# Three copies of turned attention blocks, made by ScalarE instead of VectorE, in a two-layer gated cross-attention kernel

## The chip, the core and the metric

The kernel runs on one core of one Trainium2 chip. A core has TensorE (PE in the rows; its weight loads are PEld), VectorE (DVE), ScalarE (ACT), GpSimd (POOL) and SyncE (SP, which issues most of the DMAs). Each engine works through its own list of instructions in order and waits on semaphores that other engines raise. The metric is device time in microseconds (us) of one execution, the median of several runs.

## What is computed

Two layers over `x` (2 batches, 256 rows, 128 columns), each with cross-attention to a context of 2 x 512 rows and then a feed-forward part:

```python
x = x + tanh(g_xattn[0]) * L0_xattn(layernorm(x), ctx, mask)   # 16 heads of depth 8
x = x + tanh(g_ffn[0])   * L0_ffn(layernorm(x))                # Hadamard turn, rows quantised to 4 bits, ternary weights
x = x + tanh(g_xattn[1]) * L1_xattn(layernorm(x), ctx, mask)   # 16 heads of depth 64
x = x + tanh(g_ffn[1])   * L1_ffn(layernorm(x))                # 32 experts, top 4 of them, and a shared one
```

`xattn` is `softmax(mask(q k^T / sqrt(depth))) v`, projected out. All of it is in float32.

## The kernel before

**Units.** The attention is cut into 128 units, numbered u = 0 to 127: one head, 128 query rows, all 512 context rows. Units 0 to 63 are the first layer (8 blocks of 8 units; four blocks are one batch), units 64 to 127 the second (16 blocks of 4 units). One unit passes through these steps:

1. PE computes the scores into one of two PSUM banks (`scores`, L1352 in the first layer, L1358 and L1359 in the second). Score u waits until the mask step of unit u-2 has emptied the bank.
2. DVE adds the mask and takes the row's extreme (`mask_max`, L941, two instructions); its result lies in one of three slots, so mask step u waits for the exponential of unit u-3.
3. ACT takes the exponential with its row sum (`exp`, L747, two instructions).
4. DVE takes the reciprocal of the sums (`recip`, L950).
5. POOL multiplies the rows by it (`norm`, L604).
6. PE turns the block, four 128x128 transposes into one PSUM bank (`turn`, L1227). The first layer has three such banks, so turn u waits for the copy of unit u-3.
7. The turned block is copied from PSUM into `probsT` (`copy_turned`), by DVE (L958) or by ACT (L756).

When the units of a block are copied, PE multiplies them with the values (`mix`, L1396). Below, "copy 40" is step 7 of unit 40, "mask step 40" its step 2, and so on.

**The order.** All of this is written out by hand as one list for each engine, from a loop over a step t. At step t PE makes score t+6, the jobs that `PLAN` has for t, a mix if one is due, and then turn t. DVE makes mask step t+5, reciprocal t+3, the jobs of t-1, and copy t-1 if it is DVE's; behind these come the feed-forward part and the norms. ACT makes the jobs of t-1, the exponential t+4, and copy t-1 if it is ACT's. POOL multiplies unit t+3 and has conversions, splits and norm rows behind that.

**Who copies.** Odd units are copied by ACT, even ones by DVE, except for those in a list, which ACT copies too (lines 167 and 176 to 178):

```python
MORE_ON_ACT = (36, 46, 48, 68, 70, 78, 80, 102, 110, 112)
...
def on_act(u):
    return u % 2 == 1 or u in MORE_ON_ACT
```

**The work around the change.** At t = 6 DVE has the statistics of the first norm for the second batch (`ln_stats`, L911 to L914) at the end of its step. The feed-forward part of the first batch lies at t = 37 to 47: at t = 38 its norm's statistics, at t = 41 `quantise` part 0 (L1036 to L1043, six small instructions, one behind the other), at t = 42 part 1 (L1045 to L1050). PE has mix 0 (block 0) at t = 10, mix 4 at t = 42 and mix 5 at t = 50, each ahead of that step's turn. The second layer's first projections begin at t = 49 (`k_high` by ACT, L798).

Of the kernel before, what the change touches and what calls it, by code (L numbers as in the profile page):

```python
# [163 lines left out]
BEFORE, PLAN, AFTER, NUMBER, PLACE, HIGHS = make_plan()  # L164


MORE_ON_ACT = (36, 46, 48, 68, 70, 78, 80, 102, 110, 112)
GATE_SLOTS = 4
RING = 3
LAG = 3  # L170
# [4 lines left out]
def on_act(u):  # L175

    return u % 2 == 1 or u in MORE_ON_ACT

# [1415 lines left out]
```

## Time and profile before

| | |
|---|---|
| median of 3 runs | 278.87 us (278.17 to 278.93) |
| the profiled execution | 277.44 us, of which its span is 275.4 us |
| PE busy | 252.3 us (92%) |
| DVE busy | 212.6 us (77%) |
| ACT busy | 191.6 us (70%) |
| POOL busy | 181.6 us (66%) |
| granted TensorE clock | 0.999 of full speed |

The span runs from the first to the last instruction; the 2.0 us beside it lie around it. Times in the rows count from the span's start. A row of the timeline gives the start, the duration in us, the engine, the line, the operation with output and input, and in brackets how long the engine had been idle and what it waited for. Consecutive instructions of DVE and ACT overlap a little in the records, so what an instruction costs its engine is the step from its start to the next one's start.

### The profile page before, as it was taken

The numbers are of one execution on the slowest core, as the hardware profiler recorded it, in microseconds if no ns is written. First come the engines' busy times: TensorE is split into PE (matmuls) and PEld (weight loads), VectorE is DVE, ScalarE is ACT, GpSimd is POOL, SyncE is SP. The second block draws the span as 40 slices with busy tenths as digits, with TensorE's granted clock in tenths as the row PEclk, the third lists the DMA queues.
The fourth block names the chain that finished last, engine by engine and source line by source line (L and its number), as shares of the span: only waits on it lengthen the run. The fifth ranks groups of instructions, "written<-read, shape, count | busy, mean of one in ns | idle before, by whom it ended". The sixth has DMA issues, their size and how long they took to land. (4 is left out here: it accounts for less than half of the span.)

```text
span 275.4 us, 6702 instructions
## 1 busy us (share of the span) xinstructions
PE 252.3 (92%) x1903; PEld 200.2 (73%) x1903; DVE 212.6 (77%) x654; ACT 191.6 (70%) x454; POOL 181.6 (66%) x271
## 2 busy tenths in 40 slices
PE   7897998999788999989999999999989999969694
PEld 5565666666656777768777778887757778969693
DVE  3899889889979896799677787787797536793583
ACT  3488789888788877857777676776856654853462
POOL 7367999775879765746743775348668795843380
PEclk9999999999999999999999999999999999999999
DMA  6568375200023764644585666666531221302530
GB/s 193 204 176 278 138 261 141 60 2 4 1 51 86 168 138 100 136 102 108 141 213 148 144 179 165 173 173 179 129 87 30 69 91 39 117 0 67 163 103 19
DMA packets 25987, 32.91 MB, mean 119 GB/s; under 512 B 4000, under 2 KB 18144, under 8 KB 25824
## 3 DMA queue, kind: packets, MB, share of 16 engines
q1 hardware_dynamic: 25520, 32.27, 43.4%
q8 instruction: 16, 0.26, 0.4%
q10 hardware_dynamic: 432, 0.22, 0.3%
q14 instruction: 19, 0.16, 0.2%
HBM read 14.32 MB, written 3.47 MB: 65 GB/s over the span
## 5 line engine op out<-in xcount | busy, mean ns | idle before, releaser
L604 POOL TENSOR_SCALAR probs<-probs,rsum 128x512 f32<-128x512 f32 x128 | 88.3, 697 | 57.2 <-DVE rsum L950 56.4
L747 ACT ACTIVATE probs<-masked,neg_max 128x512 f32<-128x512 f32 x128 | 91.9, 719 | 12.2 <-DVE neg_max L941 9.2
L1227 PE MATMUL bank<-ident,probs 128*128 128x128 f32 x512 | 77.9, 275 | 0.8 <-ACT probsT L756 0.8
L1227 PEld LDWEIGHTS bank<-ident,probs 128*128 128x128 f32 x512 | 60.0, 141 | 14.6 <-issue 8.2
L941 DVE CUSTOM_DVE_ANT_0 masked<-bank,mask 128x512 f32<-128x512 f32 x64 | 43.8, 685 | 15.3 <-PE bank L1359 14.6
L756 ACT ACTIVATE probsT<-bank 128x512 f32<-128x512 f32 x74 | 43.5, 589 | 16.2 <-PE bank L1227 15.8
L1396 PE MATMUL bank<-probsT,val 128*32 128x256 f32 (+1 forms) x512 | 46.6, 384 | 0.0
L958 DVE COPY probsT<-bank 128x512 f32<-128x512 f32 x54 | 36.8, 681 | 11.4 <-PE bank L1227 11.1
L941 DVE CUSTOM_DVE_ANT_0 masked<-bank,shared 128x512 f32<-128x512 f32 x64 | 43.4, 678 | 0.4 <-PE bank L1352 0.3
L1352 PE MATMUL bank<-parts 128*128 128x512 f32 x64 | 31.4, 490 | 9.0 <-DVE neg_max L941 8.8
L1396 PEld LDWEIGHTS bank<-probsT,val 128*32 128x32 f32 (+1 forms) x512 | 24.4, 123 | 17.7 <-issue 5.1
L1358 PE MATMUL bank<-k_high,q 128*128 128x512 f32 x64 | 30.6, 478 | 1.6 <-DVE neg_max L941 1.6
L648 POOL TENSOR_TENSOR q<-masked,q 128x512 fp32r<-128x512 f32 (+1 forms) x16 | 19.9, 1259 | 17.4 <-ACT q L858 17.3
L1359 PE MATMUL bank<-k_both,q 128*128 128x512 f32 x64 | 25.2, 394 | 0.0
L747 ACT ACTIVATION_READ_ACCUMULATOR probs<-masked,neg_max 128x1 f32 x128 | 24.6, 192 | 0.0
L1352 PEld LDWEIGHTS bank<-parts 128*128 128x128 f32 x64 | 12.0, 188 | 15.4 <-DVE neg_max L941 14.3
L950 DVE RECIPROCAL rsum<-sums 128x1 f32<-128x1 f32 x128 | 20.1, 158 | 0.7 <-ACT probs L747 0.7
L1179 DVE TENSOR_TENSOR bank<-bank,probsT 128x512 f32<-128x512 f32 x16 | 11.1, 694 | 8.3 <-PE bank L1234 5.6
L881 ACT ACTIVATE probsT<-bank 128x512 f32<-128x512 f32 (+1 forms) x18 | 10.2, 568 | 10.2 <-DVE masked L1192 6.6
L1016 DVE SCALAR_TENSOR_TENSOR k_low<-bank,cols,k_high 128x512 fp32r<-128x512 f32 x16 | 12.0, 749 | 6.6 <-ACT k_high L798 6.6
L798 ACT ACTIVATE k_high<-bank,cols 128x512 fp32r<-128x512 f32 x16 | 11.0, 690 | 7.4 <-PE bank L1234 7.3
L858 ACT ACTIVATE q<-masked 128x512 fp32r<-128x512 f32 (+1 forms) x18 | 10.7, 603 | 7.3 <-DVE masked L1192 6.1
(238 smaller groups left out, 524.4 us busy)
## 6 DMA issues: line engine op xcount, KB each, us to landing
k_both<-k_low SPq DMA_DIRECT2D x32, 128.0 KB, 2.8
k_both<-k_high SPq DMA_DIRECT2D x32, 128.0 KB, 2.9
q<-q_split SPq DMA_DIRECT2D x32, 128.0 KB, 2.4
probsT<-staged_gate SPq DMA_DIRECT2D x32, 128.0 KB, 3.0
q<-q_split SPq DMA_DIRECT2D x32, 64.0 KB, 2.1
parts<-staged_k SPq DMA_DIRECT2D x7, 256.0 KB, 2.7
w_flat<-in_w SPq DMA_DIRECT2D x1, 1536.0 KB, 7.6
staged_k<-k_high SPq DMA_DIRECT2D x2, 512.0 KB, 3.2
```

The source lines that it names most:

```text
L604: pool.tensor_scalar(p, p, rsum[:, u % NCOL:u % NCOL + 1], 1.0, ALU.mult, ALU.mult).then_inc(normed, 1)
L648: pool.tensor_tensor(hid_low[:, e % RING, 0:cols], hidT[:, e % RING, 0:cols], hid_high[:, e % RING, 0:cols].bitcast(F32), ALU.subtract).th ...
L747: act.activation(probs[:, u % NP, :], masked[:, u % NS, :], ACT.Exp, scale=-1.0, bias=neg_max[:, c:c + 1], accum_out=sums[:, c:c + 1]).the ...
L756: act.activation(probsT[:, k.m % 2, h, :, qt * P:qt * P + P], (turn_bank if k.layer else turn_bank0)[i][:, :].rearrange("p (k q) -> p k q" ...
L941: dve.tensor_tensor_reduce(out=masked[:, u % NS, :], in0=score_bank[u % 2][:, :], in1=mask, scale=-float(k.depth) ** -0.5, scalar=3.0e38, ...
L950: dve.reciprocal(rsum[:, c:c + 1], sums[:, c:c + 1]).then_inc(recipped, 1)
L958: dve.tensor_copy(probsT[:, k.m % 2, h, :, qt * P:qt * P + P], (turn_bank if k.layer else turn_bank0)[i][:, :] .rearrange("p (k q) -> p k ...
L1227: ins = pe.transpose(dst[0:rows, t * P:t * P + P], src, ident[:, :])
L1352: pe.matmul(dst, q0[:, k.m % 4, h, q], k0[:, k.m % 4, :], start=True, stop=True).then_inc(scored, 1)
L1358: pe.matmul(dst, q1_high[:, s, h, q], k1_high[:, s, :], start=True, stop=False)
L1359: pe.matmul(dst, q1_both[:, s, h, q], k1_both[:, s, h, :], start=False, stop=True).then_inc(scored, 1)
L1396: ins = pe.matmul(mix_bank[w * h:w * h + w, 0:SQ], v[:, i, w * h:w * h + w], probsT[:, k.m % 2, h, i, :], start=(first and i == 0), stop=( ...
```

## The change

Three more units are put on the list: copies 6, 40 and 42 are made by ACT.

```diff
-MORE_ON_ACT = (36, 46, 48, 68, 70, 78, 80, 102, 110, 112)
+MORE_ON_ACT = (6, 36, 40, 42, 46, 48, 68, 70, 78, 80, 102, 110, 112)
```

Each engine's place for copy u is the end of its step t = u + 1. ACT's list at copy 6 (bank2 holds turn 6; bank7 and bank3 hold turns 5 and 7, `probs<-masked` is an exponential):

```order
 L747 ACTIVATE probs,sums<-masked,neg_max 128x512 x2
 L756 ACTIVATE probsT<-bank7 128x4x128
-L747 ACTIVATE probs,sums<-masked,neg_max 128x512 x2
+L747 ACTIVATE probs,sums<-masked,neg_max 128x512
+L756 ACTIVATE probsT<-bank2 128x4x128
+L747 ACTIVATE probs,sums<-masked,neg_max 128x512
 L756 ACTIVATE probsT<-bank3 128x4x128
 L747 ACTIVATE probs,sums<-masked,neg_max 128x512 x2
```

Copy 6 now stands between the exponentials of units 11 and 12. ACT's list at copies 40 and 42 (bank3, bank7 and bank2 hold turns 40, 41 and 42; the last row is copy 43, from bank3 again):

```order
 L756 ACTIVATE probsT<-bank2 128x4x128
-L747 ACTIVATE probs,sums<-masked,neg_max 128x512 x2
-L756 ACTIVATE probsT<-bank7 128x4x128
-L747 ACTIVATE probs,sums<-masked,neg_max 128x512 x2
+L747 ACTIVATE probs,sums<-masked,neg_max 128x512
+L756 ACTIVATE probsT<-bank3 128x4x128
+L747 ACTIVATE probs,sums<-masked,neg_max 128x512
+L756 ACTIVATE probsT<-bank7 128x4x128
+L747 ACTIVATE probs,sums<-masked,neg_max 128x512
+L756 ACTIVATE probsT<-bank2 128x4x128
+L747 ACTIVATE probs,sums<-masked,neg_max 128x512
 L756 ACTIVATE probsT<-bank3 128x4x128
```

Copy 40 now stands between the exponentials of units 45 and 46, and copy 42 between those of units 47 and 48. DVE's list at copy 40 (bank3 is the turned block, bank6 the rows that are quantised; `ISA neg_max` closes the mask step):

```order
 L941 ISA neg_max 128x1
 L950 RECIPROCAL rsum<-sums 128x1
-L958 COPY probsT<-bank3 128x4x128
 L1036 SCALAR_TENSOR_TENSOR bank6<-mv,bank6 128x2
 L1038 TENSOR_REDUCE qs<-bank6 128x2
```

The first instruction of `quantise` now follows the reciprocal directly. The lists of PE, POOL and SP are the same as before.

## Rows read from the trace of the kernel before

**Rows 1.** The page, part 5: shapes, count | busy us, mean ns | idle before.

```profile
L756 ACT ACTIVATE probsT<-bank 128x512 f32<-128x512 f32 x74 | 43.5, 589 | 16.2 <-PE bank L1227 15.8
L958 DVE COPY probsT<-bank 128x512 f32<-128x512 f32 x54 | 36.8, 681 | 11.4 <-PE bank L1227 11.1
```

**Rows 2.** Busy time of each engine in two stretches, in us.

```profile
core 0: us, PE busy (x) PEld busy (x) DVE busy (x) ACT busy (x) POOL busy (x), PEclk, DMA share, GB/s
...
72.00:80.00 8.00, 6.71 (x59) 5.00 (x61) 7.29 (x30) 7.85 (x20) 5.73 (x9) 1.00 0.00 0
...
130.00:220.00 90.00, 88.66 (x647) 70.41 (x646) 67.95 (x212) 63.40 (x156) 56.61 (x90) 1.00 0.54 140
```

**Rows 3.** Timeline of DVE: copy 6 and mask step 13.

```profile
25.42 0.67 DVE L958 COPY probsT<-bank 128x512 f32<-128x512 f32 x1
26.00 0.68 DVE L941 CUSTOM_DVE_ANT_0 masked<-bank,shared 128x512 f32<-128x512 f32 x1
```

**Rows 4.** Timeline of ACT: exponential 12.

```profile
25.45 0.73 ACT L747 ACTIVATE probs<-masked,neg_max 128x512 f32<-128x512 f32 x1 [1.14 <-DVE neg_max L941]
```

**Rows 5.** Timeline of PE: scores 14 and 16, turn 12.

```profile
25.47 0.50 PE L1352 MATMUL bank<-parts 128*128 128x512 f32 x1 [1.02 <-DVE neg_max L941]
...
27.43 0.48 PE L1352 MATMUL bank<-parts 128*128 128x512 f32 x1
...
31.33 0.60 PE L1227 MATMUL bank<-ident,probs 128*128 128x128 f32 x4
```

**Rows 6.** Timeline of POOL: multiplications 12 and 13.

```profile
30.11 1.36 POOL L604 TENSOR_SCALAR probs<-probs,rsum 128x512 f32<-128x512 f32 x2
```

**Rows 7.** Timeline of DVE: copies 40 and 42, mask steps 47, 48, 49, `quantise`.

```profile
66.01 0.67 DVE L958 COPY probsT<-bank 128x512 f32<-128x512 f32 x1
66.60 0.16 DVE L1036 SCALAR_TENSOR_TENSOR bank<-mv,bank 128x2 f32<-128x2 f32 x1
...
68.04 0.69 DVE L941 CUSTOM_DVE_ANT_0 masked<-bank,shared 128x512 f32<-128x512 f32 x1
...
70.30 0.68 DVE L941 CUSTOM_DVE_ANT_0 masked<-bank,shared 128x512 f32<-128x512 f32 x1
...
70.99 0.67 DVE L958 COPY probsT<-bank 128x512 f32<-128x512 f32 x1
71.58 0.67 DVE L941 CUSTOM_DVE_ANT_0 masked<-bank,shared 128x512 f32<-128x512 f32 x1
```

**Rows 8.** Timeline of ACT: exponentials 46 to 49, copy 41, the first projection.

```profile
66.25 0.73 ACT L747 ACTIVATE probs<-masked,neg_max 128x512 f32<-128x512 f32 x1
...
66.96 0.60 ACT L756 ACTIVATE probsT<-bank 128x512 f32<-128x512 f32 x1
68.78 0.73 ACT L747 ACTIVATE probs<-masked,neg_max 128x512 f32<-128x512 f32 x1 [1.22 <-DVE neg_max L941]
...
71.02 0.72 ACT L747 ACTIVATE probs<-masked,neg_max 128x512 f32<-128x512 f32 x1 [1.43 <-DVE neg_max L941]
...
72.49 0.72 ACT L747 ACTIVATE probs<-masked,neg_max 128x512 f32<-128x512 f32 x1
...
78.28 0.69 ACT L798 ACTIVATE k_high<-bank,cols 128x512 fp32r<-128x512 f32 x1
```

**Rows 9.** Timeline of PE: turn 42, scores 50 and 55.

```profile
68.37 0.66 PE L1227 MATMUL bank<-ident,probs 128*128 128x128 f32 x4
...
71.04 0.50 PE L1352 MATMUL bank<-parts 128*128 128x512 f32 x1 [1.31 <-DVE neg_max L941]
...
77.03 0.50 PE L1352 MATMUL bank<-parts 128*128 128x512 f32 x1 [1.18 <-DVE neg_max L941]
```

**Rows 10.** Timeline of PE: turn 50, behind mix 5.

```profile
80.71 0.66 PE L1227 MATMUL bank<-ident,probs 128*128 128x128 f32 x4
```

**Rows 11.** Timeline of DVE: copy 50.

```profile
81.40 0.69 DVE L958 COPY probsT<-bank 128x512 f32<-128x512 f32 x1 [0.97 <-PE bank L1227]
```

**Rows 12.** The page, part 6: DMA issues, count, size, us to landing.

```profile
q<-q_split SPq DMA_DIRECT2D x32, 128.0 KB, 2.4
```

## The prediction

> **What bounds the kernel now.** I read the page first. No engine is full over the whole span (PE 92% by matmuls, DVE 77%, ACT 70%, POOL 66%), and the page's chain of waits reaches back only through the last 27 us, far behind the three copies. So what a copy is worth has to be read from the timeline of the stretch it lies in, and then followed forward.
>
> The reader should see one thing at each of the two places: DVE is working without a pause, and the others wait for its mask steps. At the first place PE had waited 1.02 us for mask step 12 before score 14 [rows 5], ACT 1.14 us before exponential 12 [rows 4], while copy 6 stands on DVE directly ahead of mask step 13 [rows 3]. At the second place `quantise` keeps DVE away from the masks: ACT waits 1.22 us for mask step 47 and 1.43 us for mask step 48 [rows 8], PE 1.31 us for mask step 48 and, further on, 1.18 us for mask step 53 [rows 9]. Later, in the second layer, PE is the bound: it is busy 88.66 of 90.00 us from 130 to 220 us [rows 2], in a fixed order. What arrives there earlier can leave earlier.
>
> **The change, part by part.**
>
> *What a copy costs.* On DVE a copy lasts 681 ns in the mean, on ACT 589 ns [rows 1]. For the engine's list the step to the next start counts: on DVE 26.00 - 25.42 = 0.58 us for copy 6 [rows 3], 66.60 - 66.01 = 0.59 us for copy 40 and 71.58 - 70.99 = 0.59 us for copy 42 [rows 7]. DVE's list gets 0.58 + 0.59 + 0.59 = 1.76 us shorter. ACT's gets at most 3 x 0.589 = 1.77 us longer. Nothing else is moved; no DMA, PE or POOL instruction changes its place. Waits are those that the copy had: its turn, and the mix that frees the buffer.
>
> *Copy 6, on ACT.* It now stands ahead of exponential 12. ACT had been idle for 1.14 us when that exponential began at 25.45 [rows 4], so from 24.31 on; a copy of 0.59 us ends by 24.90. Its cover is this idle time, and 0.55 us of it is left. Were it gone, the exponentials behind it would each come up to 0.59 us later.
>
> *Copy 6, off DVE.* Mask step 13 goes from 26.00 to 25.42. Mask step 14 then needs score 14, which starts at 25.47 behind mask step 12, unmoved, and takes 0.50 us [rows 5]: it is there at 25.97, while DVE is free for it at 25.42 + 0.68 = 26.10. So mask step 14 also comes 0.58 us earlier, and with it score 16, which waits for that mask step (27.43 to 26.85 [rows 5]). Behind it PE has mix 0 and turns 10, 11 and 12.
>
> *What is late next.* Turn 12 needs multiplication 12. POOL starts it at 30.11 with no idle time ahead of it, so it can't come earlier; two take 1.36 us, so the first is done at 30.79 [rows 6]. With about 0.1 us from there to PE (an estimate: score 50 starts at 71.04, 0.06 us behind the end of mask step 48 at 70.30 + 0.68 [rows 7, 9]), turn 12 can start at 30.9 and not at 31.33 - 0.58 = 30.75 [rows 5]. It gains 31.33 - 30.9 = 0.43 us, and so does all that stands behind it on PE. I take **0.43 us** for copy 6; the ends are 0 and 0.58.
>
> *Copies 40 and 42, off DVE.* `quantise` part 0 starts 0.59 us earlier, so mask step 47 goes from 68.04 to 67.45 and mask step 48 from 70.30 to 69.71. Without copy 42 too, mask step 49 goes from 71.58 to 70.40, that is by 1.18 us [rows 7]. PE's score 50 waits for mask step 48 and gains 0.59 us (71.04 to 70.45); score 55 waits for mask step 53 and gains the whole 1.18 us (77.03 to 75.85) [rows 9]. From there PE has a projection, turn 49, score 56, mix 5 and turn 50 in one row, so turn 50 goes from 80.71 to 79.53 [rows 10] and copy 50, for which DVE had waited 0.97 us, from 81.40 to 80.22 [rows 11].
>
> *Copies 40 and 42, on ACT.* This is the tight part. Copy 40 stands ahead of exponential 46 (66.25 [rows 8]), where ACT has no idle time: exponential 46 goes to 66.84, copy 41 from 66.96 to 67.55, and ACT is free at about 68.14. Mask step 47 now ends at 67.45 + 0.69 = 68.14 [rows 7]. So exponential 47 starts at about 68.2 and not at 68.78: the 1.22 us of idle time has been used up, half by the copy and half by the earlier mask. Copy 42 needs turn 42, which ends at 68.37 + 0.66 = 69.03 [rows 9]; exponential 47 is over at about the same time, so the copy runs from 69.1 to 69.7. Mask step 48 ends at 69.71 + 0.68 = 70.39, so exponential 48 starts at 70.43, 0.59 us earlier, with 0.7 us of idle time left. Exponential 49 then comes at 71.90 (72.49 [rows 8]). From here ACT is only 0.59 us ahead where DVE is 1.18 us ahead.
>
> *Does ACT hold the others back?* Its next work for someone else is `k_high` at 78.28 [rows 8]. At 0.59 us earlier it lets DVE's `k_low` and mask step 56 come 0.59 us earlier, and DVE then still waits 0.97 - (1.18 - 0.59) = 0.38 us for turn 50 [rows 11]. So PE's 1.18 us goes through. I take **1.18 us** for the two; the ends are 0.59 (ACT sets the pace) and 1.18.
>
> *Sum.* 0.43 + 1.18 = 1.61 us. The profiled execution of 277.44 us would become 275.8; its span of 275.4 us has 2.0 us around it that don't change. The median of the runs lies 1.43 us above it, so 278.87 - 1.61 = 277.26, **277.3 us**. Less than about 0.84 us (0.3%) can't be told from no change by a measurement of this kernel.
>
> *A rule weighed against the trace.* From 72 to 80 us ACT is busy 7.85 of 8.00 us, DVE 7.29 and PE 6.71 [rows 2]: of these, ACT is the fullest, and the change gives it work. The Trainium skill (Perfetto Trace Analysis, "Identifying the Most-Contended Engine") says to improve the engine with the highest occupancy first, so by it the two copies would go onto the wrong engine; that is the third rival. The rows of that stretch speak against it in part, since 1.22 + 1.43 us of idle time lie right ahead of it on ACT.
>
> **The rivals.**
>
> *ACT sets the pace (277.9 us).* If ACT's lead of 0.59 us is all that the second place gives, the sum is 0.43 + 0.59 = 1.02 us. For it: exponential 47 has no margin left, and ACT is full from 72 to 80 us. Against it: the 0.38 us that DVE still waits for turn 50.
>
> *The gain is lost in the second layer (278.4 to 278.9 us).* Its scores need stacked keys and queries, which come by DMAs on SP's queue, 2.4 us from issue to landing [rows 12]. If PE had been waiting on these and not on its own list, only a part up to the 0.43 us of the first place, or nothing, would be left. For it: no score of that layer can start without its stacks. Against it: the stacks follow from jobs that move with the chain, and PE is busy 98.5% of the stretch [rows 2], so it hardly waits.
>
> *Slower, ACT carries the stretch (279.1 to 280.05 us).* ACT works in order, so copies 40 and 42 each hold up the exponential behind them. If copy 42 can't start before about 70.4 (turn 42 over 1.3 us late, or exponential 47 held by a mask step that isn't earlier), the idle time is of no use, and ACT runs 2 x 0.59 = 1.18 us late [rows 1] through a stretch nearly without pauses to `k_high`. It decides once ACT is later at exponential 48 than 71.02 [rows 8]. Then up to 1.18 us goes to the end: 278.87 + 1.18 = 280.05; at the least 1.18 - 0.97 = 0.21 us, if DVE's pause in front of copy 50 takes the rest [rows 11].
>
> **How the numbers follow.** The forecast (1.2 to 1.76 us faster) 0.62, ACT's pace 0.16, lost in the second layer 0.14, slower 0.08. Faster by over 0.3%: 0.62 and about 0.11 of the 0.16, so 0.73. Slower by over 0.3%: 0.05 of the 0.08. Within: 0.22. The range reaches down to all 1.76 us less half a microsecond, as three runs of one kernel lie 0.76 us apart: 276.5; and up to the first place alone, 278.87 - 0.43 = 278.4, 278.5. That leaves out the slower case and about half of the lost one.
>
> **What would show it.** Right: mask step 13 directly behind mask step 12; copy 6 in ACT's pause; mask step 49 some 1.6 us earlier than before (0.43 and 1.18), PE's waits of 1.31 and 1.18 us shorter or the same but earlier, and turn 50 about 1.6 us earlier, a distance that then stays the same through the second layer. Wrong: a pause on DVE in front of mask step 49 or 51 with ACT as the releaser; turn 12 not earlier; exponential 48 not before 71.02; or a distance that shrinks between 90 and 130 us, which would be the second rival.

## The result, and the profile after

| | before | after |
|---|---|---|
| median, us (6 runs each) | 278.24 (277.22 to 278.93) | 275.92 (274.9 to 276.38) |
| ratio after/before, 95% interval | | 0.9923 (0.9897 to 0.995) |
| profiled execution, us | 277.44 | 275.9 |
| its span, us | 275.4 | 274.2 |

The kernel is faster by 0.5 to 1.0%: (1 - 0.9923) x 278.24 = 2.14 us, with an interval of 1.39 to 2.87 us. The sign was forecast, but 275.92 us lies below the range of 276.5 to 278.5 us. The six runs of before have the median 278.24 us, where the three runs that the prediction started from had 278.87 us. One of the later runs of before took 490.46 us, far from all others, and is left out of the medians below.

*Where the time went inside one execution.* Four rows settle it: the first mask step and the last (unit 127) in the timelines of DVE, first of before, then of after.

```profile
11.44 0.69 DVE L941 CUSTOM_DVE_ANT_0 masked<-bank,shared 128x512 f32<-128x512 f32 x1 [0.27 <-PE bank L1352]
...
216.22 0.68 DVE L941 CUSTOM_DVE_ANT_0 masked<-bank,mask 128x512 f32<-128x512 f32 x1
```

```profile
11.98 0.69 DVE L941 CUSTOM_DVE_ANT_0 masked<-bank,shared 128x512 f32<-128x512 f32 x1 [0.26 <-PE bank L1352]
...
215.08 0.68 DVE L941 CUSTOM_DVE_ANT_0 masked<-bank,mask 128x512 f32<-128x512 f32 x1
```

From the first to the last mask step before takes 216.22 - 11.44 = 204.78 us and after 215.08 - 11.98 = 203.10 us: **1.68 us less**. In this one execution 0.54 us of it is lost ahead of the first mask step (11.98 against 11.44 us), where the change has no instruction. With two decimals the spans end at 275.45 and 274.17 us, so 0.14 us is won behind the start of the last mask step (59.23 against 59.09 us) and 0.26 us outside the span (277.44 - 275.45 = 1.99 us against 275.9 - 274.17 = 1.73 us). Together that makes the 1.54 us between the two profiled executions.

*First place.* DVE (mask steps 12, 13 and 14), then ACT (exponential 11, copy 6, exponential 12), in the timeline of after:

```profile
25.27 0.68 DVE L941 CUSTOM_DVE_ANT_0 masked<-bank,shared 128x512 f32<-128x512 f32 x1
...
25.95 0.66 DVE L941 CUSTOM_DVE_ANT_0 masked<-bank,shared 128x512 f32<-128x512 f32 x1
...
26.62 0.66 DVE L941 CUSTOM_DVE_ANT_0 masked<-bank,shared 128x512 f32<-128x512 f32 x1
```

```profile
24.04 0.72 ACT L747 ACTIVATE probs<-masked,neg_max 128x512 f32<-128x512 f32 x1
...
24.77 0.57 ACT L756 ACTIVATE probsT<-bank 128x512 f32<-128x512 f32 x1
25.99 0.73 ACT L747 ACTIVATE probs<-masked,neg_max 128x512 f32<-128x512 f32 x1 [0.65 <-DVE neg_max L941]
```

Copy 6 stands in ACT's pause, which falls from 1.14 [rows 4] to 0.65 us, and mask step 13 follows mask step 12 directly. Behind it POOL (a memset, then multiplications 12 and 13) and PE (turn 12):

```profile
29.80 0.74 POOL L688 MEMSET q<- 128x768 f32 x1
30.64 1.35 POOL L604 TENSOR_SCALAR probs<-probs,rsum 128x512 f32<-128x512 f32 x2
```

```profile
31.38 0.66 PE L1227 MATMUL bank<-ident,probs 128*128 128x128 f32 x4
```

Turn 12 starts 0.06 us behind the end of the first multiplication (30.64 + 0.68 = 31.32): POOL is what it waits for now, as the prediction had it [rows 5, 6].

*Second place.* DVE (two steps of `quantise`, mask steps 47, 48 and 49, `k_low`, copy 50):

```profile
66.02 0.15 DVE L1036 SCALAR_TENSOR_TENSOR bank<-mv,bank 128x2 f32<-128x2 f32 x1
...
66.67 0.23 DVE L1039 SCALAR_TENSOR_TENSOR qs<-qs,rstd 128x2 f32<-128x2 f32 x1
...
67.53 0.69 DVE L941 CUSTOM_DVE_ANT_0 masked<-bank,shared 128x512 f32<-128x512 f32 x1
...
69.79 0.68 DVE L941 CUSTOM_DVE_ANT_0 masked<-bank,shared 128x512 f32<-128x512 f32 x1
...
70.48 0.67 DVE L941 CUSTOM_DVE_ANT_0 masked<-bank,shared 128x512 f32<-128x512 f32 x1
...
78.15 0.75 DVE L1016 SCALAR_TENSOR_TENSOR k_low<-bank,cols,k_high 128x512 fp32r<-128x512 f32 x1 [0.85 <-ACT k_high L798]
...
80.28 0.69 DVE L958 COPY probsT<-bank 128x512 f32<-128x512 f32 x1 [0.70 <-PE bank L1227]
```

ACT (copy 40, exponential 46, copy 41, exponential 47, copy 42, exponential 48, exponential 49):

```profile
66.26 0.60 ACT L756 ACTIVATE probsT<-bank 128x512 f32<-128x512 f32 x1
66.73 0.73 ACT L747 ACTIVATE probs<-masked,neg_max 128x512 f32<-128x512 f32 x1
...
67.44 0.61 ACT L756 ACTIVATE probsT<-bank 128x512 f32<-128x512 f32 x1
68.26 0.73 ACT L747 ACTIVATE probs<-masked,neg_max 128x512 f32<-128x512 f32 x1 [0.21 <-DVE neg_max L941]
...
69.07 0.60 ACT L756 ACTIVATE probsT<-bank 128x512 f32<-128x512 f32 x1
70.51 0.73 ACT L747 ACTIVATE probs<-masked,neg_max 128x512 f32<-128x512 f32 x1 [0.85 <-DVE neg_max L941]
...
71.98 0.72 ACT L747 ACTIVATE probs<-masked,neg_max 128x512 f32<-128x512 f32 x1
```

PE (score 55):

```profile
75.93 0.50 PE L1352 MATMUL bank<-parts 128*128 128x512 f32 x1 [1.11 <-DVE neg_max L941]
```

The pauses of 1.22 and 1.43 us ahead of exponentials 47 and 48 [rows 8] have become 0.21 and 0.85 us, with DVE's mask still the releaser: ACT still waits for DVE at both. The groups of the page and the busy time of the two stretches:

```profile
L756 ACT ACTIVATE probsT<-bank 128x512 f32<-128x512 f32 x77 | 45.3, 589 | 16.2 <-PE bank L1227 15.9
L958 DVE COPY probsT<-bank 128x512 f32<-128x512 f32 x51 | 34.7, 680 | 11.1 <-PE bank L1227 10.8
```

```profile
core 0: us, PE busy (x) PEld busy (x) DVE busy (x) ACT busy (x) POOL busy (x), PEclk, DMA share, GB/s
...
72.00:80.00 8.00, 6.89 (x69) 5.13 (x67) 6.62 (x26) 8.00 (x21) 6.29 (x10) 1.00 0.00 0
...
130.00:220.00 90.00, 88.34 (x645) 70.08 (x644) 67.52 (x208) 62.93 (x155) 56.71 (x90) 1.00 0.56 141
```

Three copies have changed engines, 74 to 77 and 54 to 51 [rows 1]. ACT is now busy for all of the 8 us that the prediction watched (7.85 before [rows 2]), and the kernel is faster nevertheless; from 130 to 220 us PE is as full as before.

### The profile page after: what moved, and what is told of

Same layout as the page of the kernel before. It is cut to its first block and busy times, and to the rows that moved or that the text cites. A ratio compares the mean times of both kernels' runs of the same rounds, so it can differ in the third digit from the quotient of the medians.

```text
span 274.2 us, 6702 instructions
## 1 busy us (share of the span) xinstructions
PE 252.3 (92%) x1903; PEld 200.4 (73%) x1903; DVE 210.9 (77%) x651; ACT 192.7 (70%) x457; POOL 181.0 (66%) x271
## 5 line engine op out<-in xcount | busy, mean ns | idle before, releaser
L756 ACT ACTIVATE probsT<-bank 128x512 f32<-128x512 f32 x77 | 45.3, 589 | 16.2 <-PE bank L1227 15.9
L958 DVE COPY probsT<-bank 128x512 f32<-128x512 f32 x51 | 34.7, 680 | 11.1 <-PE bank L1227 10.8
```

The lines of the kernel that those rows point to most:

```text
L756: act.activation(probsT[:, k.m % 2, h, :, qt * P:qt * P + P], (turn_bank if k.layer else turn_bank0)[i][:, :].rearrange("p (k q) -> p k q" ...
L958: dve.tensor_copy(probsT[:, k.m % 2, h, :, qt * P:qt * P + P], (turn_bank if k.layer else turn_bank0)[i][:, :] .rearrange("p (k q) -> p k ...
```

## The experiments

The theory: the gain is made at the two places, in the sizes that the sum gave, and the rest of the distance to the forecast is scatter between executions. Rivals: a third place, ACT at its limit, POOL as a cap beyond what was counted.

The edits touch one list and, in some kernels, one line of POOL's; a diff is against the changed kernel, while the table names what the list has beyond the old one. Since one median says little at this size, a second measure is used beside it: the start of a step less the start of mask step 0 in the same execution, and from that the same difference in the profile of before. Negative is earlier, in us:

| kernel (added to the list) | mask 13 | turn 12 | mask 40 | mask 47 | mask 49 | turn 50 | mask 64 | mask 127 |
|---|---|---|---|---|---|---|---|---|
| e1_null (nothing) | -0.01 | -0.01 | 0.00 | 0.01 | 0.00 | -0.01 | -0.03 | -0.02 |
| after (6, 40, 42) | -0.60 | -0.50 | -0.53 | -1.05 | -1.65 | -1.67 | -1.68 | -1.68 |
| e2_again (6, 40, 42) | -0.60 | -0.50 | -0.53 | -1.05 | -1.64 | -1.66 | -1.67 | -1.66 |
| e3_only6 (6) | -0.60 | -0.49 | -0.53 | -0.53 | -0.53 | -0.54 | -0.55 | -0.55 |
| e4_only40_42 (40, 42) | -0.01 | -0.01 | 0.00 | -0.51 | -1.10 | -1.13 | -1.15 | -1.19 |
| e5_memset (6, 40, 42) | -0.61 | -0.62 | -0.63 | -1.15 | -1.74 | -1.74 | -1.75 | -1.92 |
| e6_copy14 (6, 14, 40, 42) | -0.60 | -0.60 | -1.22 | -1.73 | -2.33 | -2.34 | -2.35 | -2.29 |
| e7_more44 (6, 40, 42, 44) | -0.60 | -0.49 | -0.53 | -1.05 | -1.64 | -1.33 | -1.32 | -1.50 |
| e8_double42 (6, 40, 42) | -0.59 | -0.49 | -0.52 | -1.04 | -1.63 | -1.66 | -1.68 | -1.90 |
| e9_14_pool (6, 14, 40, 42) | -0.59 | -0.47 | -1.09 | -1.60 | -2.19 | -2.21 | -2.23 | -2.21 |
| e10_best (as e6) | -0.60 | -0.60 | -1.19 | -1.70 | -2.29 | -2.31 | -2.33 | -2.29 |

The first row is the old kernel profiled again: up to 0.03 us in these columns, the measure's own error. One jump of 0.2 us at unit 119, which the last section tells of, comes on top of it in three kernels.

### The kernel before, once more (e1_null)

```diff
-MORE_ON_ACT = (6, 36, 40, 42, 46, 48, 68, 70, 78, 80, 102, 110, 112)
+MORE_ON_ACT = (36, 46, 48, 68, 70, 78, 80, 102, 110, 112)
```

> The kernel before, unchanged, against itself. Every theory expects a ratio of 1.000; what it differs from that, and how far the time to the first mask step moves between executions (11.4 us in the profile before, 12.0 us in the profile after), is what run-to-run difference alone makes. If the start-up theory holds (the 0.4 to 0.6 us by which the measured gain of about 2.1 us is above my 1.61 us are scatter of the start and of the median of before), single runs here scatter by 1 us or more and the two medians lie up to 0.5 us apart. If the extra gain is a real effect of the change, they lie within 0.2 us.

Measured: 278.65 us (276.77 to 279.11, 11 runs) against 277.80 us for before on that chip (27 runs), ratio 1.0025 (1.0003 to 1.0048). A kernel compared with itself comes out 0.69 us away by the ratio, so a gap of that size between medians is no evidence. Nor is an interval that just leaves out 1, since this one does and nothing was changed. The profiles show where it can come from. In the eleven profiles of this study other than that of before, the first mask step starts between 11.10 and 12.33 us, in no relation to the edits, the span goes on for 58.61 (e4) to 60.02 us (e1) from the start of the last mask step, and 1.7 to 2.7 us lie outside the span.

### The change, once more (e2_again)

No edit.

> The changed kernel once more. Theory of the places (copy 6 gives 0.53 us, copies 40 and 42 give 1.13 us, as the two profiles show, and little else counts): 1.7 us faster, ratio 0.994. Rival (the change gives more outside these places, in the start, the tail or around the span): 2.1 us or more again, ratio 0.9925 or less. From the first mask step to the last instruction both expect the profile's 1.9 us.

Measured: 276.1 us (6 runs), ratio 0.9941 (0.9923 to 0.996), or 1.64 us of 277.80 us, where the first measurement gave 2.14 us. The interval takes in both the 0.994 of the theory and the 0.9925 of the rival, so the ratio alone doesn't decide. The distances repeat within 0.02 us; from the first mask step to the end of the span it is 1.67 us less than in before, not the 1.9 us expected.

### Copy 6 alone, and copies 40 and 42 alone (e3_only6, e4_only40_42)

```diff
-MORE_ON_ACT = (6, 36, 40, 42, 46, 48, 68, 70, 78, 80, 102, 110, 112)
+MORE_ON_ACT = (6, 36, 46, 48, 68, 70, 78, 80, 102, 110, 112)
```

> Only copy 6 goes to ACT. Theory of the places: 0.5 us faster (0.43 by my sum, 0.53 by the profile after), cut short by POOL's multiplication 12 at turn 12, and the same 0.5 us at every unit from 20 to 127; ratio 0.998. Rival (the first place counts for nothing, since something later takes it back): 0.0 us at units 30 to 40. Rival (POOL does not limit): 0.58 us or more at turn 12.

```diff
-MORE_ON_ACT = (6, 36, 40, 42, 46, 48, 68, 70, 78, 80, 102, 110, 112)
+MORE_ON_ACT = (36, 40, 42, 46, 48, 68, 70, 78, 80, 102, 110, 112)
```

> Only copies 40 and 42 go to ACT. Theory of the places: 1.1 to 1.2 us faster from mask step 49 on, kept to unit 127; ratio 0.996. Rival, ACT sets the pace: 0.5 to 0.6 us at turn 50 and after, ratio 0.998. Rival, ACT carries the stretch: no gain or slower.

Measured: e3 277.24 us, ratio 0.9983 (0.9962 to 1.0003), 12 runs; e4 276.48 us, 0.9957 (0.9933 to 0.9981), 12 runs. By ratio that is 0.47 and 1.19 us, and e3 can't be told from no change by it. The distances say the same more sharply: 0.55 us from copy 6 and 1.13 us at turn 50 from the other two (1.19 at unit 127), together 1.68 to 1.74 us, against 1.66 to 1.68 us for all three. The two places are independent and add up, and up to unit 127 there is no third.

### POOL's memsets out of the way (e5_memset)

```diff
-                if t in (8, 10):
-                    publish_late(pool.memset(q1_high[:, :, t // 10, :].bitcast(F32), 0.0))
+                if t in (27, 35):
+                    publish_late(pool.memset(q1_high[:, :, t // 35, :].bitcast(F32), 0.0))
```

> The changed kernel, with POOL's two memsets of the second layer's queries moved from t = 8 and 10, just ahead of multiplications 12 and 14, to t = 27 and 35, where POOL has idle time. Theory (POOL's multiplication 12 cuts the gain of copy 6 from 0.58 to 0.50 us at turn 12): turn 12 and all behind it come 0.07 to 0.1 us earlier than in the changed kernel, counted from the first mask step. Rival (something else cuts it): turn 12 stays where it is, 0.0 us. Both: the median can't tell it.

In the changed kernel turn 12 waits for POOL, and the memset of 0.74 us stands ahead of multiplication 12. Both memsets go to later steps. Measured: 275.87 us (10 runs), ratio 0.9933 (0.9908 to 0.9959). POOL's multiplications 11 to 13 now stand in one row, in the timeline of e5:

```profile
28.27 2.03 POOL L604 TENSOR_SCALAR probs<-probs,rsum 128x512 f32<-128x512 f32 x3
```

Turn 12 goes from -0.50 to -0.62 us, mask step 40 from -0.53 to -0.63. So the cap that the prediction put on copy 6 is real and costs 0.1 us.

### A copy in the next such pause (e6_copy14, e9_14_pool, e10_best)

The edit of e6 and e10, with the memsets moved as in e5; e9 has the list alone:

```diff
-MORE_ON_ACT = (6, 36, 40, 42, 46, 48, 68, 70, 78, 80, 102, 110, 112)
+MORE_ON_ACT = (6, 14, 36, 40, 42, 46, 48, 68, 70, 78, 80, 102, 110, 112)
```

> The kernel of the moved memsets, and copy 14 by ACT too. A copy that DVE makes at t = 15 between the second batch's projections and its values, in a stretch where DVE does not pause. Theory (a copy taken from DVE where PE waits for its mask steps is worth its 0.59 us): score 24 and mix 1 come 0.4 to 0.6 us earlier than in the kernel without it, and so does unit 127. Rival (POOL, which does not pause from 25 to 42 us, is the bound there): turn 22 waits for multiplication 22, 0.0 to 0.1 us.

> The changed kernel and copy 14 by ACT, but with POOL's two memsets where they were (t = 8 and 10). It tells what POOL's lateness costs. Theory: counted from the first mask step, score 24 and mix 1 come 0.6 us earlier than in the changed kernel, turn 22 is held by multiplication 22 and gains only 0.0 to 0.2 us, and what of the 0.6 us is left at unit 30 tells whether that hold is on the path: between 0.1 (all of it) and 0.6 us (copy 22, its only user, has idle time ahead of it).

> The fastest version so far once more, with more rounds: copies 6, 14, 40 and 42 by ACT and the memsets at t = 27 and 35. Theory: 2.3 us faster than before from the first mask step to unit 127, as in the first run of it, ratio 0.992. Rival (its ratio was scatter): 0.994, as for the changed kernel.

Measured: e6 275.5 us, ratio 0.9923 (0.989 to 0.9955), 9 runs; e9 275.58 us, 0.9913 (0.9887 to 0.9938), 6 runs; e10 275.96 us, 0.9922 (0.9898 to 0.9946), 6 runs. Copy 14 brings 0.6 us more in the distances (mask step 40 from -0.63 in e5 to -1.22), the slot of one copy, and keeps it (mask step 64 from -1.75 to -2.35). At unit 127 only 0.37 us of it show, since e5 has the jump of 0.2 us at unit 119 and e6 doesn't. In e9, without the moved memsets, turn 22 waits for its multiplication, which doesn't start earlier than before. PE and POOL in the timeline of e9:

```profile
43.16 0.66 PE L1227 MATMUL bank<-ident,probs 128*128 128x128 f32 x4 [0.46 <-POOL probs L604]
```

```profile
42.42 1.36 POOL L604 TENSOR_SCALAR probs<-probs,rsum 128x512 f32<-128x512 f32 x2
```

At that turn only 0.48 us of the distance is there (0.52 us in after), but at turn 26 it is 1.09 us (turn 20 had 0.99): the hold lies off the path. All three have copies 6, 14, 40 and 42 on ACT and are faster than before by 0.8 to 0.9%. That they beat the changed kernel (0.9923 and 0.9941) rests on the distances, since the intervals overlap.

### One copy more on ACT (e7_more44)

```diff
-MORE_ON_ACT = (6, 36, 40, 42, 46, 48, 68, 70, 78, 80, 102, 110, 112)
+MORE_ON_ACT = (6, 36, 40, 42, 44, 46, 48, 68, 70, 78, 80, 102, 110, 112)
```

> The changed kernel, and copy 44 by ACT too, ahead of exponential 50, where ACT has no pause. It tells whether ACT or DVE sets the pace between 70 and 80 us. Rival (ACT, the fullest engine there, sets the pace): exponentials 50 to 53 about 0.5 us later than in the changed kernel, and turn 50 and unit 127 0.3 to 0.5 us later. Theory (PE behind DVE's mask steps sets the pace up to turn 50): exponentials 0.2 to 0.5 us later, but score 55 0.3 to 0.6 us earlier, and unit 127 between 0 and 0.4 us earlier.

Measured: 276.34 us (10 runs), ratio 0.9958 (0.9929 to 0.9986). My theory, a gain of up to 0.4 us, fell: at turn 50 the kernel has -1.33 us where the changed one has -1.67. DVE now waits for exponentials, in the timeline of e7 (reciprocals, then `k_low`):

```profile
72.53 0.17 DVE L950 RECIPROCAL rsum<-sums 128x1 f32<-128x1 f32 x1 [0.16 <-ACT probs L747]
...
73.72 0.17 DVE L950 RECIPROCAL rsum<-sums 128x1 f32<-128x1 f32 x1 [0.38 <-ACT probs L747]
...
78.35 0.75 DVE L1016 SCALAR_TENSOR_TENSOR k_low<-bank,cols,k_high 128x512 fp32r<-128x512 f32 x1 [0.90 <-ACT k_high L798]
```

At the two reciprocals DVE doesn't wait in after, and `k_low` comes 0.49 us later than there, each counted from its first mask step (78.35 - 11.69 = 66.66 against 78.15 - 11.98 = 66.17 us). ACT has become the engine that others wait for, one copy past the change.

### The price of copy 42 on ACT doubled (e8_double42)

```diff
+                if u == 42:
+                    act.activation(x1_high[:, :].rearrange("p (k q) -> p k q", q=P),
+                                   turn_bank0[i][:, :].rearrange("p (k q) -> p k q", q=P), ACT.Copy)
```

The block is copied a second time, into a buffer that isn't in use then.

> The changed kernel, but ACT copies turn 42 twice, first into a buffer that is free at that time, then as before: the cost of copy 42 on ACT is doubled. Theory: ACT has 0.8 us of idle time ahead of exponential 48 left, the second copy takes 0.5 to 0.6 us of it, and nothing moves behind it: 0.0 us at exponential 48, turn 50 and unit 127. Rival (ACT's added copies cost part of the gain): 0.3 to 0.6 us later from exponential 48 on.

Measured: 276.25 us (8 runs), ratio 0.9945 (0.9923 to 0.9967). ACT in the timeline of e8, where the lines count up to three more (the added copy, copy 42, exponential 48):

```profile
69.43 0.60 ACT L757 ACTIVATE x_high<-bank 128x512 fp32r<-128x512 f32 x1
69.92 0.59 ACT L759 ACTIVATE probsT<-bank 128x512 f32<-128x512 f32 x1
70.87 0.73 ACT L747 ACTIVATE probs<-masked,neg_max 128x512 f32<-128x512 f32 x1 [0.35 <-DVE neg_max L944]
```

The pause ahead of exponential 48 falls from 0.85 to 0.35 us, and no step from 40 to 58 moves by more than 0.02 us against e2. So ACT does not set the pace at copy 42, and 0.35 us of its cover are still left with the price doubled. The -1.90 us at unit 127 (-1.68 in after) isn't the second copy's: e5, e7 and e8 all gain 0.2 us at unit 119, and the last section shows in what.

## Why the prediction was right and wrong

**The step that failed is the start of the sum.** "The median of the runs lies 1.43 us above it, so 278.87 - 1.61 = 277.26" treats a median of three runs as the place from which to subtract, and the low end of 276.5 lay only 0.76 us under the result of that. That median was high: six runs gave 278.24 us, and in the three later comparisons before had 277.80, 277.6 and 278.14 us. A kernel against itself is off by 0.69 us (e1). The high start makes 0.63 of the 1.34 us between 277.26 and 275.92 us: from 278.24 us the same sum gives 276.63 us, inside the range. Of the 0.71 us that are left, 0.07 us is the sum's own error (below), and the rest did not come again, since e2 had 276.1 us where 277.80 - 1.61 gives 276.19 us. It is of the size of the scatter; no run shows more of its cause. The text had the other way in hand: the profiled execution "would become 275.8", which is 0.1 us from its 275.9 and from the median of 275.92 us. The agreement with 275.9 is partly luck, since +0.54 us ahead of the first mask step, -0.14 us behind the last one and -0.26 us outside the span nearly cancel; "2.0 us around it that don't change" did change. The range should have taken in that whole difference of 1.43 us between two executions of one kernel; the argument for its width, that "three runs of one kernel lie 0.76 us apart", used the smaller of the two distances that were there to see.

**The sum was right.** Forecast 0.43 + 1.18 = 1.61 us, measured 1.68 us from the first mask step to unit 127, 1.66 us in e2.

- *Slots of a copy.* DVE lost 0.58 to 0.59 us each, as read. On ACT the price was taken from the record, 0.589 us, and was too high: the step from start to start is 66.73 - 66.26 = 0.47 us. The two profiles are level here, as the 0.54 us lost ahead of the first mask step and the 0.53 us won at the first place cancel, so absolute times compare: exponential 46 starts at 66.73, 0.48 us behind the 66.25 of [rows 8] and not 0.59; and exponential 47, which was to have nothing left, has 0.21 us. The tight part was less tight than it was told.
- *Copy 6.* Mask step 13 at -0.60 (forecast -0.58). "What is late next" named POOL, and that was right (e5); its term was a little small, 0.43 against 0.50 us at turn 12, for the most part because the handover from POOL to PE took 0.06 us and not 0.1. The 0.53 us at mask step 40 and 0.55 us at the second layer (e3) are not explained by that.
- *Copies 40 and 42.* At mask step 47 they bring 0.52 us (1.05 - 0.53), not 0.59; the rest went into one small instruction (below). Mask step 49 has -1.12 us, turn 50 -1.14, against a forecast of 1.18 (e4: 1.10 and 1.13).
- *Pass through ACT.* `k_high` frees `k_low` with 0.85 us of waiting, and copy 50 still waits 0.70 us for its turn (0.97 before [rows 11]): the bound there stayed with PE, as the forecast had it, by more than the 0.38 us that it counted. ACT was further ahead there than the 0.59 us of the text: e4 has `k_high` 0.87 us earlier than before, counted from the first mask step.

**The rivals.** *ACT sets the pace* fell: e8 doubles a copy there at no cost. It is the truth one copy further (e7). *Lost in the second layer* fell: the distance is -1.68 us at unit 64 and at unit 127. *Slower* fell: exponential 48 starts at 70.51, before the 71.02 [rows 8] from which that case was to decide.

*The rule weighed against the trace* was read on the wrong stretch. From 72 to 80 us ACT is the fullest, but copies 40 and 42 begin at 66.01 and 70.99 us [rows 7], and from 66 to 72 us DVE is the fullest and ACT is busy 3.35 of 6.00 us, in before:

```profile
66.00:72.00 6.00, 4.69 (x53) 3.09 (x50) 5.72 (x23) 3.35 (x10) 3.89 (x7) 1.00 0.02 5
```

The columns are those of [rows 2]. The rule of the Trainium skill (Perfetto Trace Analysis, "Identifying the Most-Contended Engine") is to improve the engine with the highest occupancy first. In the copies' own stretch that is DVE, and the trace agrees (1.1 us gained by relieving it). It agrees for the next copy too: copy 44 starts on ACT at 72.39 us in e7, in the full stretch, and 0.34 us is lost at turn 50 (1.67 - 1.33).

## What to carry to other kernels

Move an instruction off the engine whose results others wait for, into a pause of another engine that lies directly ahead in its list, and price it by the step from start to start; what counts is whom the others wait for in the stretch where the instruction stands, not which engine is fuller in a later one. Then follow the gain to the next instruction that doesn't move, here POOL's multiplication. A gain of half a per cent should be read from a fixed step inside the trace, and a range set around it should take in how far whole executions of the unchanged kernel lie apart.

## What was not expected of the hardware

The instruction L1039 of `quantise`, on 2 elements per partition, took 0.16 us where POOL was idle, and 0.23 us where it fell beside a multiplication on POOL. The rows are DVE in before, POOL in after (DVE's row of after stands above, at the second place), and DVE in e3 and e4:

```profile
67.25 0.16 DVE L1039 SCALAR_TENSOR_TENSOR qs<-qs,rstd 128x2 f32<-128x2 f32 x1
```

```profile
65.53 1.37 POOL L604 TENSOR_SCALAR probs<-probs,rsum 128x512 f32<-128x512 f32 x2 [0.57 <-DVE rsum L950]
```

```profile
66.97 0.16 DVE L1039 SCALAR_TENSOR_TENSOR qs<-qs,rstd 128x2 f32<-128x2 f32 x1
```

```profile
66.50 0.23 DVE L1039 SCALAR_TENSOR_TENSOR qs<-qs,rstd 128x2 f32<-128x2 f32 x1
```

In after it starts at 66.67, inside POOL's row, and both end at 66.90; in before POOL is idle from 66.89 on. It is 0.16 us in before, e1 and e3, and 0.23 to 0.24 us in after, e2 and all of e4 to e10, where it ends with POOL's multiplication within 0.02 us. These 0.07 us are what mask step 47 lacks. L1036, an instruction of the same form with one input in a PSUM bank, takes 0.15 us in after, inside the same row of POOL.

The jump of 0.2 us in e5, e7 and e8 is of the same kind. It lies between mask steps 118 and 119 (-1.73 and -1.95 us in e5), where the steps L1118 to L1121 on DVE stand beside POOL's L610, which makes a part of `w_early`. DVE and POOL in before, then in e5:

```profile
200.56 0.73 DVE L1118 TENSOR_TENSOR_SCAN small<-ones,small 128x32 f32<-128x32 f32 x2
```

```profile
200.82 0.41 POOL L610 TENSOR_SCALAR w_early<-we 128x256 fp32r<-128x256 f32 x1
```

```profile
198.49 0.48 DVE L1118 TENSOR_TENSOR_SCAN small<-ones,small 128x32 f32<-128x32 f32 x2
```

```profile
198.75 0.45 POOL L610 TENSOR_SCALAR w_early<-we 128x256 fp32r<-128x256 f32 x1
```

In all twelve profiles POOL's instruction starts 0.02 to 0.03 us ahead of the second L1118. In nine of them that L1118 then takes 0.45 us and POOL's 0.40 to 0.41; in e5, e7 and e8 it takes 0.19 us and POOL's 0.45. From the first L1118 to L1122 it is 1.86 us in before and 1.64 us in e5. No edit goes with it, since e6 and e10 contain e5's edit and don't have it.

That POOL is the cause was not tried in either place; only the coincidence is shown.
